# A transformer layer on one core: zeros for the dispatch table and normalised rows written in parts, expert weights loaded in pairs, all qkv jobs ahead of the first tile, attention's end two tiles up

## What is computed

```python
def _gate(hs, gate_weight, bias):            # 16 experts in 4 groups, 2 groups kept, 6 experts a row
    scores = jax.nn.sigmoid(hs @ gate_weight.T)
...
for e in range(E):
    g = hs @ gate_proj[e].T
    u = hs @ up_proj[e].T
    inter = jax.nn.silu(g) * u
    out = out + comb[:, e:e + 1] * (inter @ down_proj[e].T)
...
shared_out = jax.nn.silu(sg) * su @ shared_down_w.T
```

## Time and profile before

| | us |
|---|---|
| median of 3 runs | 500.22 (497.48 to 501.37) |
| the profiled execution | 500.93 |
| its span | 499.1 |
| PE busy | 415.1 |
| DVE busy | 361.3 |
| ACT busy | 224.7 |
| POOL busy | 237.3 |
| DMA moved | 91.55 MB, mean 183 GB/s |

### The profile page before, as it was taken

One profiled execution on the slowest core, in us unless ns is written; L12 is line 12 of the kernel. 1 busy time (PEld: TensorE's weight loads), 2 busy tenths in 40 slices (PEclk: granted clock), 3 DMA queues, 4 the chain that ended last, 5 costly groups with the idle time before them and its releaser, 6 DMA issues.

```text
span 499.1 us, 7322 instructions
## 1 busy us (share of the span) xinstructions
PE 415.1 (83%) x1981; PEld 318.4 (64%) x1981; DVE 361.3 (72%) x585; ACT 224.7 (45%) x609; POOL 237.3 (48%) x223
## 2 busy tenths in 40 slices
PE   5599987998377999989899999999999999998000
PEld 5597976777255777767667777767766677676000
DVE  2537693277469999999899998999943255589831
ACT  3445323224325444554466665664456544644000
POOL 2611212475767777777200000006377777575772
PEclk9596988899779999999899999999999999999555
DMA  7999999324245666655333323336467996563633
GB/s 193 338 350 351 362 414 367 109 91 167 90 156 168 207 201 213 195 185 168 100 99 97 110 87 106 103 98 172 142 180 204 248 237 177 161 185 115 193 109 87
DMA packets 65733, 91.55 MB, mean 183 GB/s; under 512 B 8224, under 2 KB 57120, under 8 KB 65440
## 3 DMA queue, kind: packets, MB, share of 16 engines
q1 hardware_dynamic: 53920, 63.02, 40.8%
q0 software_dynamic: 9216, 25.96, 17.1%
q10 hardware_dynamic: 2560, 2.10, 1.6%
HBM read 43.48 MB, written 47.57 MB: 182 GB/s over the span
## 4 chain that ended last, share of the span: by engine, by line
PE 48%; DVE 18%; DMA 13%; issue 7%; POOL 6%; ACT 4%; SPq 2%; DVEq 1%; POOLq 0%
PE gate L897 17%; PE ps_y L920 15%; DMA xs_dram<-xrow,slot_i 11%; PE up L887 3%; POOL xs_dram L536 3%; PE ps_y L913 3%; DVE prod L996 3%; DVE qkv L996 3%; PE misc L947 2%; PE gate L833 2%; DVE inter_s L1407 1%; DVE yacc L1489 1%; DVE sc L996 1%; SPq L381 1%; PE up L833 1%
## 5 line engine op out<-in xcount | busy, mean ns | idle before, releaser
L897 PE MATMUL gate<-wrec,xgT 128*128 x444 | 152.4, 466 | 0.9 <-issue 0.6
L536 POOL DMA_INDIRECT xs_dram<-xrow,slot_i x96 | 112.3, 1169 | 60.4 <-DMA xs_dram<-xrow,slot_i 31.0
L920 PE MATMUL ps_y<-wrec,interT 88*128 x444 | 119.2, 391 | 9.0 <-ACT interT L667 4.5
L555 POOL DMA_INDIRECT gat<-y_dram,slot_i x57 | 64.4, 1129 | 130.1 <-DMA y_dram<-y_s 98.5
L920 PEld LDWEIGHTS ps_y<-wrec,interT 88*128 88x128 f32 x444 | 81.1, 190 | 50.9 <-issue 31.1
L897 PEld LDWEIGHTS gate<-wrec,xgT 128*128 128x128 f32 x444 | 76.7, 193 | 26.2 <-issue 2.9
L1407 DVE SCALAR_TENSOR_TENSOR inter_s<-gate,xg,gate_s 128x176 f32<-128x176 f32 x111 | 43.7, 394 | 41.1 <-ACT gate_s L660 35.4
L680 ACT ACTIVATE y_s<-ps_y 128x256 f32<-128x256 f32 x107 | 41.1, 384 | 69.2 <-PE ps_y L920 67.7
L660 ACT ACTIVATE gate_s<-gate 128x176 f32<-128x176 f32 x111 | 35.2, 318 | 62.4 <-PE gate L897 61.8
L887 PE MATMUL up<-ident,xg 128*128 128x128 f32 x222 | 43.5, 277 | 11.9 <-DMA xg<-xs_dram 11.9
L887 PEld LDWEIGHTS up<-ident,xg 128*128 128x128 f32 x222 | 31.6, 143 | 24.1 <-DMA xg<-xs_dram 12.6
(11 more groups left out here) (198 smaller groups left out, 626.7 us busy)
## 6 DMA issues: line engine op xcount, KB each, us to landing
xs_dram<-zrow SPq DMA_DIRECT2D x1, 15096.0 KB, 50.9
xg<-xs_dram SPq DMA_DIRECT2D x111, 136.0 KB, 2.4
y_dram<-y_s SPq DMA_DIRECT2D x111, 128.0 KB, 1.7
wrec<-wexp SPq DMA_DIRECT2D x14, 608.0 KB, 14.4
xn_dram<-xrow SPq DMA_DIRECT2D x8, 256.0 KB, 10.1
qkv<-xn_dram SPq DMA_DIRECT2D x8, 256.0 KB, 4.9
xs_dram<-xrow,slot_i POOLq DMA_INDIRECT x96, 2.9
wrec<-wexp SPq DMA_DIRECT2D x1, 1216.0 KB, 5.8
```

The lines of the kernel that those rows point to most:

```text
L536: nc.gpsimd.indirect_dma_start(xs_dram, bass.IndirectOffsetOnAxis(slot_i[:, o:o + 1], 0), xw[:, c, :], None).then_inc(sent[n % LANES], 16)
L555: nc.gpsimd.indirect_dma_start(places[place_of(n)][:, there:there + H], None, y_dram[0:DONE[max(d for d in DONE if d <= first)] * P, :], b ...
L897: last = nc.tensor.matmul(guA[t % 2][:, 0:2 * I], xgT[:, t % 2, k * P:(k + 1) * P], wrec[:, bass.ds(record + k * 2 * I, 2 * I)], start=(k ...
L920: last = nc.tensor.matmul(ps_y[:, t % 2 * 2 * H:t % 2 * 2 * H + H], interT[:, t % 2, k * P:(k + 1) * P], wrec[0:HALF, bass.ds(record + KT ...
```

## The change

Four things, in the words of the code:

- **Zeros in parts.** `zero_tiles` fills only the first DONE[0] = 69 tiles of `xs_dram` from SBUF, and a small `z_dram` of ZT = 3 tiles beside it. The tiles from 69 on are filled by `copy_zeros`, a DMA from `z_dram` to `xs_dram` of 3 tiles (408 KB). Six of these go out after the weights, with waits for units (`m_ok` 9, 9, 10, 10, 11, 11), and eight in tiles 4 to 11. POOL waits for `first_zeros` ahead of the first scatter, for `more_zeros` ahead of scatter 54 and for `last_zeros` ahead of scatter 72. A scatter's target is cut to the tiles that its row group can reach.
- **Weights in pairs behind units.** The 14 experts' loads are issued two at a time, when DVE has done units 2, 3, ... 8 (`m_ok` 3 to 9).
- **Normalised rows in parts.** The 8 stores to `xn_dram` move from ahead of the tiles to tiles 19 to 26, one each.
- **Order.** `columns(0)` on PE moves behind the last qkv job. The second half of the attention transposes starts at tile 85 (was 86), the reading of `xn_dram` at 85 (87), the projections at 89 (91) and the normalisation at 98 (100).

```diff
-                 86: (8, 9), 87: (10, 11), 88: (12, 13), 89: (14, 15)}
-XN_AT = 87
-PROJECTIONS_AT = {91 + j: (j,) for j in range(8)}
-NORM_AT = 100
+                 85: (8, 9), 86: (10, 11), 87: (12, 13), 88: (14, 15)}
+XN_AT = 85
+XN_OUT_AT = 19
+ZEROS_AT = 4
+ZT = 3
+PROJECTIONS_AT = {89 + j: (j,) for j in range(8)}
+NORM_AT = 98
...
+        def zero_tiles(engine, t0, t1, done):
+            engine.dma_start(xs_dram[t0 * P:t1 * P, :].rearrange("(t p) w -> p t w", p=P),
+                             zrow[:, :].unsqueeze(1).to_broadcast([P, t1 - t0, XW])).then_inc(done, 16)
+        def copy_zeros(engine, t, done):
+            engine.dma_start(xs_dram[t * P:(t + ZT) * P, :], z_dram).then_inc(done, 16)
+        def zeros_left(engine):
+            for done in (first_zeros, spare_zeros):
+                engine.wait_ge(done, 16)
...
-            sp.dma_start(xs_dram.rearrange("(t p) w -> p t w", p=P), zrow[:, :].unsqueeze(1).to_broadcast([P, NT, XW])
-                         ).then_inc(fill_out, 16)
-            for e in range(TAIL):
-                sp.dma_start(wrec[:, e * REC:(e + 1) * REC], wexp[:, e * REC:(e + 1) * REC]).then_inc(w_in, 16)
-            sp.wait_ge(xn_ok, C)
-            for run, b, r in lane_runs():
-                sp.dma_start(by_lane(xn_dram, b, r), xw[run, :, 0:H]).then_inc(xn_out, 16)
+            zero_tiles(sp, 0, DONE[0], first_zeros)
+            sp.dma_start(z_dram.rearrange("(t p) w -> p t w", p=P), zrow[:, :].unsqueeze(1).to_broadcast([P, ZT, XW])
+                         ).then_inc(spare_zeros, 16)
+            for u in range(2, 2 + TAIL // 2):
+                sp.wait_ge(m_ok, u + 1)
+                for e in (2 * u - 4, 2 * u - 3):
+                    sp.dma_start(wrec[:, e * REC:(e + 1) * REC], wexp[:, e * REC:(e + 1) * REC]).then_inc(w_in, 16)
+            sp.wait_ge(spare_zeros, 16)
+            for n, t in enumerate(range(DONE[0], DONE[MARKS[1]], ZT)):
+                sp.wait_ge(m_ok, 2 + TAIL // 2 + n // 2)
+                copy_zeros(sp, t, more_zeros)
...
+                if t - ZEROS_AT in range(0, (NT - DONE[MARKS[1]]) // ZT):
+                    copy_zeros(sp, DONE[MARKS[1]] + (t - ZEROS_AT) * ZT, last_zeros)
+                if t - XN_OUT_AT in range(2 * 4):
+                    run, b, r = lane_runs()[t - XN_OUT_AT]
+                    sp.dma_start(by_lane(xn_dram, b, r), xw[run, :, 0:H]).then_inc(xn_out, 16)
...
-            pool.wait_ge(fill_out, 16)
+            pool.wait_ge(first_zeros, 16)
...
+                if n == MARKS[1] * TOP:
+                    pool.wait_ge(more_zeros, 16 * ((DONE[MARKS[1]] - DONE[0]) // ZT))
+                if n == MARKS[2] * TOP:
+                    pool.wait_ge(last_zeros, 16 * ((NT - DONE[MARKS[1]]) // ZT))
...
-                if n == QKV_JOBS - 2:
-                    columns(0)
+            columns(0)
             columns(1)
```

More of the change, by code:

```diff
@@ L535, in _ @@
                 o = c * KEEP + k
-                nc.gpsimd.indirect_dma_start(xs_dram, bass.IndirectOffsetOnAxis(slot_i[:, o:o + 1], 0), xw[:, c, :], None
+                nc.gpsimd.indirect_dma_start(xs_dram[0:DONE[max(d for d in DONE if d <= c)] * P, :],
+                                             bass.IndirectOffsetOnAxis(slot_i[:, o:o + 1], 0), xw[:, c, :], None
                                              ).then_inc(sent[n % LANES], 16)
@@ L639, in _ @@
             act.wait_ge(d_ok, UNITS)
-            act.wait_ge(fill_out, 16)
+            zeros_left(act)
             act.wait_ge(rows_ok, 2)
@@ L1508, in _ @@
             y_sum(NBLK - 1)
-            dve.wait_ge(fill_out, 16)
+            zeros_left(dve)
             for i in range(AHEAD - sum(HEADS_PLAN.values())):
```

4 lines of the change are left out of this document (3 added, 1 removed).

## The result

| | before | after |
|---|---|---|
| median of the runs | 499.41 us (497.48 to 501.37, 4 runs) | 516.11 us (515.04 to 517.87, 4 runs) |
| profiled execution, span | 500.93, 499.1 | 515.04, 513.0 |
| granted TensorE clock, mean | 0.913 | 0.903 |

The ratio is 1.0338, 95% interval 1.0285 to 1.0391: slower by 16.7 us. I had forecast 505.7 and a range up to 512. The sign was right, and the size was three times too small. Before's profiled execution, at 500.93, is 3 to 4 us longer than the medians of the same kernel in the later comparisons on three other chips, 496.9 to 497.8.

A forecast was written before the change was run, and what follows sets the result against it. TensorE's tiles and the chain of scatters releasing them were taken to bound the kernel; +5.5 + 1.0 - 0.5 - 0.5 = +5.5 on 500.93 gave 506.4, as a median 505.7 us, range 495.5 to 512.

The forecast's parts named there:

- The mechanism up to the 30th scatter: 30th scatter and tile 0's load move by 11.6 + 4.5 - 10.6 = +5.5 us, the load from 136.5 to about 142.
- the eight copies beside tiles 4 to 11: Copies of zeros issued where three scatters may be in flight: 1.0 us in all, bounds 0 to 8.
- the stretch from the 54th to the 96th scatter: No term of its own; the last scatter, issued at 237.93 before, was expected near 244.
- Four pairs: Weight pairs behind units 5 to 8 fall among the scatters: 2.9 us each, 11.6 in all, bounds nothing to 12.1.
- Six copies: Copies of zeros among the scatters when units 8 to 10 end: 4.5 us, from nothing to 12.2.
- What was removed: Normalised rows' stores leave the first eight scatters' stretch, where they and the weights lost 10.6 us: -10.6.
- The chain loses about as long as SP's queue moves bytes: Scatter chain before tile 0: 10.6 us lost for 12.2 of transfer, 2.9 lost for 3.0 at 410 GB/s.
- the gaps behind units 5 to 8: Sign: four gaps of 4 us or more between scatters there, smaller ones behind units 9 and 10.
- The rival that a scatter slips between the packets of a load: Scatters from 77 to 112 us: 0.7 us a pair, total -5.8, about 494.5; chance 0.15.
- Taken back at tile 39 or at tile 15: Tile 0's 2.5 us gain from jobs first is lost waiting for later scatters: 0 in total, bounds -2.5 to 0.
- Attention's end: Transposes, projections and normalisation moved up, one sum less among DVE's later additions: -0.5 us, between -2 and +1.
- The rows' stores: Normalised rows' 2 MB moved beside tiles 19 to 26: 0 us there, bound 5.

The follow-up runs named there:

- whole fill: Changed kernel with all 111 tiles' zeros filled at once from SBUF and none of the 14 DRAM-to-DRAM copies: 499.19 us, ratio 1.003 to the kernel before.
- 14 copies early: Changed kernel with all 14 copies of zeros issued right behind the fill, weight pairs unchanged: 499.66 us, ratio 1.0003 to the kernel before.
- six copies early: Changed kernel with the six early copies of zeros right behind the fill, the eight beside tiles 4 to 11 kept: 511.57 us, ratio 1.0296 to before.
- three in flight: Kernel before with tile 0's columns behind the last job, attention's end moved up, and FLIGHT_AHEAD 3 instead of 2: 487.41 us, ratio 0.979.
- jobs first: Kernel before with one edit, tile 0's columns behind the last qkv job: 495.51 us, ratio 0.9946.
- attention's end: Kernel before with only the second half of the attention transposes one tile up, and row reading, projections and normalisation two up: 496.42 us, ratio 0.9986.
- all ahead: Changed kernel with SP's fill, normalised rows, 14 weights and 14 copies issued one behind the other, nothing beside the tiles: 496.08 us, ratio 0.9988 to before.
- rows early: Changed kernel with the eight stores of normalised rows right behind the fill instead of beside tiles 19 to 26: 512.33 us, ratio 1.0288 to before.
- weights at once: Changed kernel with all 14 experts' weights issued right behind the fill without waits for units, copies unchanged: 502.49 us, ratio 1.0094 to before.
- copies by rows: Changed kernel with each copy of zeros written as 384 pieces of 1088 bytes instead of pieces of 26112 bytes: 512.31 us, ratio 1.0322 to before.
- small shift: Changed kernel plus a memset of about 0.1 us on POOL before each of scatters 86 to 93: 513.8 us, ratio 1.0348 to before.

## Why the prediction was right or wrong

The mechanism up to the 30th scatter was right, and everything behind it was priced at 1.0 us, where 11.2 us of lag arose. Two steps failed: the eight copies beside tiles 4 to 11, and the stretch from the 54th to the 96th scatter, which was taken to be as long as before.

**The chain up to the 30th scatter: right in sum (+5.5, measured +4.8), less sure in its terms.** Four pairs: 11.6 predicted, 13.4 measured, or 11.9 against the other profile with the same first stretch. Six copies: 4.5 predicted; the profiles with no copies there are shorter by 5.8 (64.2 - 58.4, whole fill), 3.1 (61.1, 14 early) and 1.5 (62.7, six early), so the size is open. What was removed: 10.6 predicted. No run has neither pairs nor copies among the scatters; by subtraction such a stretch would take 45.0 to 49.3 (an estimate: 64.2 - 13.4, less 5.8 or 1.5), so before's 59.4 held about 10 to 14. The sum may thus owe something to errors that cancel. "The chain loses about as long as SP's queue moves bytes" holds for the pairs: 3.0 to 3.35 us each for 3.0 of transfer at 410 GB/s. Tile 0's load went out at 142.59, as forecast. Of the signs I named, the gaps behind units 5 to 8 are there (5.62, 3.62, 4.86 and 6.86 us from scatter to scatter); the one behind units 9 and 10, which I had called smaller, is 4.55.

The rival that a scatter slips between the packets of a load, which the Trainium skill suggests by its turn-taking between queues ("DMA: Bandwidth & Descriptors", section "Queues, rings and completion order"), is not what happened: a pair costs 3.0 to 3.35 us, its full length. The rows: the waits of 4.65, 3.90 and 3.90 us above, behind units 5, 7 and 8 (the one behind unit 6 is 2.67; the two of 3.58 stand behind copies and the last weights). How the DMA engines share their time between the queues, no run here separates.

**The eight copies in tiles 4 to 11: the step that failed first.** I priced them at 1.0, with a bound of 8. They cost 4.6 in the scatters from the 30th to the 54th (41.4 against 36.8; over all profiles 40.5 to 45.2 with these copies and 36.2 to 38.1 without, 34.9 with three in flight), about 2 more in the next six, and 12 to 15 us in the total. My reason for the low price was that the DMA engines are only half busy there and that three scatters may be in flight. That was the wrong measure: here landings came late, and POOL's chain stood for them, with three in flight and with DMA engines that had time to spare on the average. (That a landing is late by the copy, the load and the store that SP asks for at once is my reading; the runs show that it is late when the copies are there.) POOL's timeline of the changed kernel shows the longest such wait, which begins at 168.2; SP's shows the copy ahead of it, then the seventh copy and the late tile load:

```profile
170.62 0.95 POOL L571 DMA_INDIRECT xs_dram<-xrow,slot_i  x1 [2.43 <-DMA xs_dram<-xrow,slot_i]
```

```profile
167.05 0.50 SPq L390 DMA_DIRECT2D xs_dram<-z_dram  x1
...
178.03 0.48 SPq L390 DMA_DIRECT2D xs_dram<-z_dram  x1
185.08 0.32 SPq L462 DMA_DIRECT2D xg<-xs_dram  x1
```

From 171 to 182 there are four more waits of over 0.4 us for a landing, of 0.47, 1.37, 1.04 and 0.67 us (one of 1.43 stands ahead of the first copy, which goes out at 162.45); in the same scatters (44 to 54) of before POOL waits for no landing. The load at 185.08 is tile 15's, which SP would otherwise have issued right behind the copy at 178.03; it needs the 54th scatter, issued at 181.52. PE stood 2.92 us and then ran at a granted clock of 0.72 for the 6 us from 187. I had named tile 15 as a place where a gain might be taken back, and never priced a loss there.

**The stretch from the 54th to the 96th scatter: not in the sum at all.** I let the last scatter be late by what the 30th is late. It took 5.4 longer. Between the two profiles this falls as follows: 2.1 in scatters 54 to 60, beside the eighth copy (185.94) and the loads that tile 15's had held up; 0.7 in 60 to 72; 2.0 in 72 to 85, beside the stores of the normalised rows, which I had priced at 0 with a bound of 5; and 0.5 in 85 to 96.

Behind the last figure stands something that I had misread. In eight of the 13 profiles five or six issues in a row take 2.27 us instead of 0.96, one per tile of 2.58 us. Before's profile has five of them, from 227.62 to the one in the earlier trace rows, the changed kernel's has six, and so they hardly count in the difference of these two. But the 85th to the 96th scatter takes 21.7 to 25.6 us with them and 15.1 to 16.9 without. I read the row as POOL's work at this place, "2.27 of work and 0.30 of idle". In fact it is one of two rhythms:

| kernel | slow issues | 54th to 96th | PE's wait at tile 39 |
|---|---|---|---|
| jobs first | none near the end | 63.7 | none |
| attention's end | none near the end | 62.3 | none |
| all ahead | none near the end | 60.8 | none |
| three in flight | none near the end | 61.0 | none |
| six copies early | none | 68.1 | 1.65 |
| before, profiled | 92 to 96 | 67.1 | 1.78 |
| whole fill | 90 to 95 | 71.3 | 4.71 |
| rows early | 88 to 93 | 71.3 | 7.90 |
| 14 copies early, profiled | 88 to 93 | 71.7 | 6.62 |
| after | 88 to 93 | 72.5 | 7.73 |
| weights at once | 86 to 91 | 75.4 | 9.70 |
| copies by rows | 86 to 91 | 74.7 | 10.27 |
| small shift | 86 to 91 | 73.7 | 10.40 |

POOL in the version with six copies early, in the same part of the program:

```profile
241.61 0.96 POOL L570 DMA_INDIRECT xs_dram<-xrow,slot_i  x1 [0.30 <-issue]
242.88 1.01 POOL L570 DMA_INDIRECT xs_dram<-xrow,slot_i  x1 [0.31 <-issue]
```

and DVE's tile product in that version, then in the changed kernel:

```profile
241.53 0.39 DVE L1441 SCALAR_TENSOR_TENSOR inter_s<-gate,xg,gate_s 128x176 f32<-128x176 f32 x1
...
244.11 0.39 DVE L1441 SCALAR_TENSOR_TENSOR inter_s<-gate,xg,gate_s 128x176 f32<-128x176 f32 x1
```

```profile
234.62 0.39 DVE L1442 SCALAR_TENSOR_TENSOR inter_s<-gate,xg,gate_s 128x176 f32<-128x176 f32 x1
...
237.20 0.39 DVE L1442 SCALAR_TENSOR_TENSOR inter_s<-gate,xg,gate_s 128x176 f32<-128x176 f32 x1
```

In the quick rhythm two issues fit between two products (0.96 + 0.30 + 1.01 + 0.30 = 2.57 of 2.58 us) and none is under way when a product starts. In the slow one an issue starts 1.22 us after a product (235.84 after 234.62), is under way when the next starts (237.20), and ends at 238.11; the next starts again 1.22 us behind a product (238.42). As long as nothing else comes between, each rhythm goes on as it is. The Trainium skill, page "SBUF — State Buffer", section "Who interferes with whom", says that VectorE and GpSimd hold a shared pair of ports by an exclusive lock, and that a VectorE tensor-tensor operation with both inputs in SBUF contends with GpSimd's reads. The same section says that such operations were not seen to stall DMAs. The 1.3 us by which an issue is longer is about the 1.21 us of such an operation beside it, which would fit the first and not the second; no run separates the two, and what starts the slow rhythm stays open. What the runs show is where it is found: in none of the profiles in which PE does not wait at tile 39, and in all but one of those in which it does.

**"Taken back at tile 39 or at tile 15": right for the changed kernel, wrong as a rule.** From the load to tile 0's product it is 7.3 us in the changed kernel and 9.65 before, the 2.4 us that the jobs first were to give. But PE then waits 2.92 us at tile 15 and 7.73 at tile 39 for loads that follow the 54th and the 96th scatter, and between 150 and 185 us POOL waits for no tile product but only for landings (behind that for products by 0.9 us in one place). So, as far as the profile shows, what PE won at tile 0 it stood longer there, and the 0 in the sum was right. What is wrong is that the last scatter always bounds: I had taken the 1.78 us of one profiled execution for a bound that always stands. In the four profiles of the table in which the last stretch takes 60.8 to 63.7 us, PE has no such wait.

**Attention's end (-0.5): right as far as the noise lets one see. The rows' stores (0): wrong by about 2 us of the chain, inside the bound of 5.** POOL's waits for tile products (-0.5) fell from 2.7 to 1.2 us, which makes no difference beside the rest. The tail behind the last product takes 41.8 us for 42.8, as said "within 1 us".

**Why so large a change cost and did not gain.** The fill's last 5.85 MB (42 tiles of 136 KB), the weights and the rows were mostly hidden work before: SP's queue was over at about 93 us, when only the first eight scatters had met it. Parting them into pairs, copies and stores behind units and tiles moved them out of a stretch in which nobody waited and into the path of scatters 3 to 85.

In sum, in PE's time: the lag of 15.0 at tile 40 is 3.8 from tile 0 (its load 6.1 late, 1.4 of it by the first scatter, less the gain of the jobs first), 3.9 from tile 15, 0.5 before tile 20, and 6.8 from tile 39 (a wait 5.95 longer, and behind it 6 us at a granted clock of 0.61 where before had 0.72). The tail gives 1.0 back, which makes 14 of the 14.1 between the two profiled executions. The medians are 16.7 apart because before's profiled execution was 1.5 above its median and the changed kernel's 1.1 below. Of the 15.0 only the first step stood in the prediction, which let it through to the end and added 1.0 for all the rest; the two steps behind it, 4.4 and 6.8, are what it lacked.

## What to carry to other kernels

Give a queue its bulk transfers in one row at the earliest moment at which the engines are free, and look at the DMA share of the stretch that the bytes leave and of the one they go to; the mean share is no cover for a chain of dependent small transfers, which here lost the full length of every pair of weights. Before moving transfers around such a chain, allow it one more in flight: here that single number (with two edits that alone gave 0.5% and 0.1%) gave 2.1%, more than any order of the queue. And in a chain with several marks (30, 54, 96), price each mark's stretch by itself, since a loss at a later mark is added and not covered.

## What was not expected of the hardware

- A third scatter in flight took the chain of 29 scatters from 59.4 to 51.1 us beside the same transfers, though a landing with little traffic beside it takes 2.4 us, no more than the time of two issues (2 x 1.27). All of the 8.3 us were saved where weights or rows moved beside the chain (scatters 1 to 9 and 21 to 30), none from the 9th to the 21st.
- The same indirect issue takes 0.96 or 2.27 us on GpSimd, five or six of the long issues in a row, each started 1.21 to 1.23 us after VectorE's product of a tile in the profiles looked at (before, whole fill, 14 copies early, after, small shift).
- From DRAM to DRAM the 14 copies ran at about 328 GB/s (with everything of SP's queue at once, 6.00 MB of that queue from 74.0 to 92.3 us), where the weights move at about 410: slower, but not half. Asked for early, the same copies cost nothing in the total, so their rate is not the cause of the loss.
